# Two graph layers on one core: layer 0's softmax steps for two groups at once, and layer 1's running sums through TensorE and ScalarE

## The reference, cut to what matters

```python
# layer 0, per edge (row, col), 8 heads of 32
scores = sum(Q[row] * K[col], -1) / sqrt(32) * cutoff
attn   = softmax(scores, over the 8 heads)
aggr   = segment_sum(xn[col] * w_phys + gate * attn * V[col], row)      # then @ wo
# layer 1, per edge, 4 heads of 64
e   = leaky_relu(h_l[row] + h_r[col], 0.2)
m   = segment_max(e, row)
ex  = exp(e - m[row])
out = segment_sum(ex * h[col], row) / (segment_sum(ex, row) + 1e-16)
```

## Time and profile before

| | us |
|---|---|
| median of three runs | 2322.39 |
| lowest, highest | 2319.65, 2326.3 |
| the profiled execution, its own time | 2321.69 |
| its span, first to last instruction | 2319.9 |

### The profile page before, as it was taken

One profiled execution on the slowest core, in us unless ns is written; L12 is line 12 of the kernel. 1 busy time (PEld: TensorE's weight loads), 2 busy tenths in 40 slices (PEclk: granted clock), 3 DMA queues, 4 the chain that ended last, 5 costly groups with the idle time before them and its releaser, 6 DMA issues.

```text
span 2319.9 us, 42068 instructions
## 1 busy us (share of the span) xinstructions
PE 1961.0 (85%) x9839; PEld 1426.4 (61%) x9840; DVE 1784.6 (77%) x4372; ACT 1479.1 (64%) x5220; POOL 1409.6 (61%) x1393
## 2 busy tenths in 40 slices
PE   5999999999958899998988889837777877877874
PEld 3777777777747677777777777624444444544542
DVE  5655444444359999998999999667999989999987
ACT  1585555555567777777777777446666666666660
POOL 0377777666776666665666664247666666666660
PEclk9999999999989999999999999977999989998997
DMA  8534444333389888888889882034433333343311
GB/s 279 160 133 144 157 146 146 138 138 131 113 291 301 299 290 292 298 293 280 296 290 308 291 296 76 19 93 113 110 107 107 105 108 100 105 110 104 106 32 56
DMA packets 162185, 403.69 MB, mean 174 GB/s; under 512 B 46887, under 2 KB 59099, under 8 KB 162108
## 3 DMA queue, kind: packets, MB, share of 16 engines
q0 software_dynamic: 79360, 276.09, 36.8%
q1 hardware_dynamic: 82748, 126.67, 17.4%
HBM read 343.89 MB, written 84.72 MB: 185 GB/s over the span
## 4 chain that ended last, share of the span: by engine, by line
PE 39%; DVE 28%; issue 16%; DMA 8%; ACT 4%; DVEq 4%; POOL 2%; SPq 0%; ACTq 0%; POOLq 0%
PE ps L1405 15%; DMA arena<-sorted_edges 6%; DVE gmx L1297 5%; PE ps L1391 4%; PE ps L1518 3%; PE ps L1521 3%; DVE arena L1329 3%; PE ps L1456 3%; PE ps L1533 2%; DVE work L1292 2%; DVE sc L1139 2%; DVE arena L1125 2%; DVEq L350 2%; PE ps L1643 2%; DVE arena L1132 2%
## 5 line engine op out<-in xcount | busy, mean ns | idle before, releaser
L630 POOL DMA_INDIRECT arena<-node_row,idxC x464 | 485.6, 1047 | 233.2 <-issue 136.8
L563 POOL DMA_INDIRECT sorted_edges<-work,pos_i x416 | 405.5, 975 | 236.5 <-issue 118.9
L1405 PE MATMUL ps<-w_sb,arena 128*128 128x256 f32 x1664 | 388.7, 386 | 0.2 <-ACT arena L674 0.2
L1643 PE MATMUL ps<-arena,hq 128*128 128x260 f32 x928 | 279.3, 428 | 96.2 <-DVE work L1292 92.8
L1069 DVE TENSOR_TENSOR work<-ps,b_bc 128x512 f32<-128x512 f32 x208 | 143.6, 691 | 273.6 <-PE ps L1405 273.6
L1405 PEld LDWEIGHTS ps<-w_sb,arena 128*128 128x128 f32 x1664 | 307.5, 190 | 72.2 <-issue 32.5
L585 POOL DMA_INDIRECT work<-node_kvx,idxB x232 | 245.7, 1059 | 154.4 <-DVE arena L1156 54.2
L585 POOL DMA_INDIRECT arena<-node_kvx,idxB x232 | 244.1, 1052 | 144.2 <-issue 51.2
L684 ACT ACTIVATE work<-work 128x256 f32<-128x256 f32 x416 | 187.5, 500 | 209.5 <-DVE work L1069 209.4
L1518 PE MATMUL ps<-arena,work 128*128 128x256 f32 x928 | 256.5, 400 | 59.1 <-issue 52.1
L1297 DVE TENSOR_REDUCE gmx<-ps 128x4 f32<-128x1024 f32 x232 | 282.5, 1218 | 28.4 <-PE ps L1618 28.4
(11 more groups left out here) (216 smaller groups left out, 3786.1 us busy)
## 6 DMA issues: line engine op xcount, KB each, us to landing
arena<-sorted_edges SPq DMA_DIRECT2D x232, 260.0 KB, 4.7
work<-sorted_rows SPq DMA_DIRECT2D x58, 256.0 KB, 3.6
arena<-in_edge_attr SPq DMA_DIRECT2D x25, 512.0 KB
node_kvx<-arena SPq DMA_DIRECT2D x24, 384.0 KB, 2.5
arena<-node_row,idxC POOLq DMA_INDIRECT x464, 3.3
sorted_edges<-work,pos_i POOLq DMA_INDIRECT x416, 2.5
sorted_edges<-arena SPq DMA_DIRECT2D x25, 260.0 KB
sorted_edges<-arena SPq DMA_DIRECT2D x1, 6240.0 KB
```

The costliest lines, as they stand in the source:

```text
L563: pool.indirect_dma_start(rec_dram[:, :], bass.IndirectOffsetOnAxis(ap=pos_i[:, 4 * q + c:4 * q + c + 1], axis=0), recA[:, q % 8, c, :], N ...
L630: pool.indirect_dma_start(row1_g[:, st.slot(16), j, :], None, row1_dram[:, :], bass.IndirectOffsetOnAxis(ap=idxC[:, batch(st).slot(4), st. ...
L1405: ins = pe.matmul(ps[:, 5 + t, half * H:(half + 1) * H], hidT[:, r, m, half, t * P:(t + 1) * P], w2_sb[:, m, :], start=m == 0, stop=m == 1)
L1643: ins = pe.matmul(agg1[r], oneh1[:, r16, j, :], msg1[:, r, j, :], start=j == 0, stop=j == GJ - 1)
```

## The change

Layer 0: `reciprocal`, the attention product and the maximum run once for two groups (an even step takes the maximum of the pair, the odd step after it the other two), the four exponentials of a pair come together on ScalarE in every second step, `msgA` and the final sum come one step later, the rings of the small tiles grow from two to four, and `msgP` gets a ring of four (two slots lie in tiles that are no longer read). The tile numbers are loaded four at a time, twice in a turn, instead of eight at once. Loading a record waits for ScalarE's scaling also.

Layer 1: VectorE no longer adds to `acc1` and no longer scales it. TensorE adds the accumulator itself, as a third matmul with the identity into the same PSUM tile; ScalarE copies the result back, and where the group is the last of a batch it does so in four pieces of 65 columns, each scaled by the next batch's `mscale`. TensorE and ScalarE now load tile numbers for this, VectorE no longer does. VectorE makes the one-hot matrix of a group's second half in one instruction; ScalarE makes the first half alone. `msg1` has a ring of eight. TensorE sums with a lag of 15 (13 before), ScalarE copies with a lag of 17.

```diff
-        def tiles_of(eng, k, lag, count=8):
+        def tiles_of(eng, k, lag, first):
             _, values = nc.values_load_multi_w_load_instructions(
-                gt_i[0:1, bass.ds(k * 8 + (16 - lag), count)], ...
+                gt_i[0:1, bass.ds(k * 8 + (FRONT - lag + first), 4)], ...
 ...
             def load_rec(st):
                 if not st.first(8):
                     sp.wait_ge(s("msgP_ready"), st.n - 7)
+                    sp.wait_ge(s("qk_cut"), st.n - 7)
 ...
             # ScalarE, layer0
-                e = st.back(4)
-                if e.real():
+                if st.u % 2 and st.back(4).real():
+                    e = pair0(st.back(4))
                     act.wait_ge(s("sc_ready"), e.n + 1)
 ...
-                    for j in range(GJ):
-                        ins = act.activation(pe_[:, r, j, :], sc[:, r, j, :], ACT.Exp, ...
+                    for r in (st.back(5).slot(4), st.back(4).slot(4)):
+                        for j in range(GJ):
+                            ins = act.activation(pe_[:, r, j, :], sc[:, r, j, :], ACT.Exp, ...
 ...
             # ScalarE, layer1
+                if st.u % 8 == 0:
+                    act_tiles[17] = tiles16(ACT_ENGINE, st.k, 17, st.u // 8)
+                d = st.back(17)
+                if d.real():
+                    act.wait_ge(s("agg1_ready"), d.n + 1)
+                    to = acc1[:, bass.ds(act_tiles[17][st.u % 8], 1), :].rearrange("p a n -> p (a n)")
+                    if d.u % BG == BG - 1 and not d.end():
+                        k = batch(d).back(-1)
+                        act.wait_ge(s("mscale"), k.n + 1)
+                        for h in range(NH1):
+                            ins = act.activation(to[:, h * HE:(h + 1) * HE], agg1[d.slot(2)][:, h * HE:(h + 1) * HE],
+                                                 ACT.Copy, scale=mscale[:, k.slot(2), h:h + 1])
+                        ins.then_inc(s("acc1_done"), 1)
+                    else:
+                        act.copy(to, agg1[d.slot(2)]).then_inc(s("acc1_done"), 1)
 ...
-                    for j in range(GJ):
-                        act.activation(away[:, st.slot(2), j, :], iota1[:, :], ACT.Abs, ...
+                    act.activation(away[:, h.slot(2), 0, :], iota1[:, :], ACT.Abs, ...
 ...
             # VectorE, layer0: lags a 3, b 4, m 5, c 7 (before: a 3, b 4, c 6)
+                if not both_in and b.real():
+                    e = pair0(b)
+                    re = m.slot(4)
+                    dve.wait_ge(s("exp0"), e.n + 1)
+                    dve.reciprocal(prec[:, :, :], psum_[:, re:re + 2, :]).then_inc(s("prec"), 1)
 ...
+                if both_in and a.real():
+                    r0 = b.slot(4)
                     dve.wait_ge(s("qk_cut"), na + 1)
-                    dve.tensor_reduce(smax[:, ra, :], sc[:, ra, :, :], AX.X, ALU.max, negate=True).then_inc(
-                        s("sc_ready"), 1)
+                    dve.tensor_reduce(smax[:, r0:r0 + 2, :], sc[:, r0:r0 + 2, :, :], AX.X, ALU.max,
+                                      negate=True).then_inc(s("sc_ready"), 1)
 ...
             # VectorE, layer1
-                    tiles[8] = tiles16(DVE, st.k, 11, 0)
 ...
-                    dve.tensor_tensor(acc, acc, agg1[c.slot(2)], ALU.add).then_inc(
-                        s("acc1_done"), 1)
 ...
+                    dve.tensor_scalar(oneh1[:, st.slot(16), 1, :], iota1[:, :], srcC[:, b.slot(4), g, 1:2], None,
+                                      ALU.is_equal)
 ...
             # TensorE, layer1
+                if st.u % 8 == 0:
+                    pe_tiles[15] = tiles16(PE, st.k, 15, st.u // 8)
+                d = st.back(15)
 ...
+                    if not d.first(1):
+                        pe.wait_ge(s("acc1_done"), n)
+                    pe.matmul(agg1[r], ident[:, :],
+                              acc1[:, bass.ds(pe_tiles[15][st.u % 8], 1), :].rearrange("p a n -> p (a n)"),
+                              start=False, stop=True).then_inc(s("agg1_ready"), 1)
```

More of the change, by code:

```diff
@@ L56, in real, with end @@
         return not isinstance(self.k, int) or 0 <= self.n < self.total
+    def end(self):
+        return isinstance(self.k, int) and self.n == self.total - 1
     def first(self, count):
@@ L156, in gnn_kernel @@
         ones = sb("ones", [P, P])
-        w1_sb = sb("w1_sb", [P, H])
+        mlp_only = sb("mlp_only", [P, 4, H])
+        w1_sb, b2_bc, lnw_bc, lnb_bc = (mlp_only[:, i, :] for i in range(4))
         w2_sb = sb("w2_sb", [P, 2, H])
@@ L276, in gnn_kernel @@
                       for v in (NT * (H + HR), NT * (H + HR) + NB * ME))
+        at_same = NT * (H + HR) + 2 * NB * ME
+        same = work[:, at_same:at_same + NB]
         apart = carve(NB * ME * ME).rearrange("p (b e f) -> p b e f", b=NB, e=ME)
@@ L379, in batch, with pair0, msgP_of @@
             return Step(st.k, st.u // BG, 16 // BG, NB)
+        def pair0(st):
+            return Step(st.k, st.u // 2, 4, NG // 2)
+        def msgP_of(st):
+            r = st.slot(4)
+            return msgP[:, r, :, :] if r < 2 else mlp_only[:, 2 * r - 4:2 * r - 2, :]
         def pair(st):
@@ L804, in _ @@
             act.wait_ge(s("hr_parts"), 2)
+            act.wait_ge(s("same"), 1)
             act_tiles = {}
@@ L863, in layer1 @@
                                  own.rearrange("p a q n -> p (a q) n")).then_inc(s("hl_set"), 1)
-                e = b.back(3)
-                if g == 0 and e.real():
+                e = b.back(2)
+                if g == 3 and e.real():
                     r = e.slot(2)
@@ L871, in layer1 @@
                     act.wait_ge(s("mdiff"), e.n + 1)
-                    if not e.first(2):
-                        act.wait_ge(s("acc1_scaled"), e.n - 1)
-                    act.activation(mscale[:, r, :], mdiff[:, r, :], ACT.Exp).then_inc(s("mscale"), 1)
-            run(act, NG, 16, 9, layer1)
+                    act.activation(mscale[:, r, :], mdiff[:, r, :], ACT.Exp,
+                                   scale=same[:, bass.ds(e.n, 1)]).then_inc(s("mscale"), 1)
+            run(act, NG, 16, 17, layer1)
         @block.vector
@@ L1158, in layer0 @@
+                if m.real():
+                    if not both_in:
+                        dve.wait_ge(s("attn"), pair0(m).n + 1)
+                    if not m.first(2):
+                        dve.wait_ge(s("agg0_ready"), m.n - 1)
+                    dve.tensor_tensor(heads(msgA[:, m.slot(2), :, :]), heads(kvx_g(m)[:, :, H:2 * H]),
+                                      attn[:, m.slot(2), :, :].unsqueeze(3).to_broadcast([P, GJ, NH0, HD0]),
                                       ALU.mult).then_inc(s("msgA_ready"), 1)
-                if a.real():
+                if both_in and a.real():
+                    r0 = b.slot(4)
@@ L1326, in layer1 @@
                         dve.wait_ge(s("exp1"), batch(m).n + 1)
-                    if not m.first(2):
-                        dve.wait_ge(s("agg1_ready"), m.n - 1)
-                    dve.tensor_tensor(msg1[:, m.slot(2), :, :].rearrange("p c (h d) -> p c h d", d=HE),
+                    if not m.first(8):
+                        dve.wait_ge(s("msg1_used"), m.n - 7)
+                    dve.tensor_tensor(msg1(m).rearrange("p c (h d) -> p c h d", d=HE),
                                       row1_g[:, m.slot(16), :, 0:HR].rearrange("p c (h d) -> p c h d", d=HE),
```

155 lines of the change are left out of this document (71 added, 84 removed).

## The result

The changed kernel takes 2434.41 us (median of four runs, 2432.01 to 2440.77), the kernel before 2322.38 us (four runs beside it): ratio 1.0485, 95% interval 1.0469 to 1.0501. It is slower by 112 us; forecast were 2231 us.

The account below looks back on a forecast made before the run. VectorE was taken to lead both layers, with TensorE close to the bound in layer 0. From 2321.7 us, 56 saved in layer 0 and 39 in layer 1, with 4 lost at the end, gave 2231 us; range 2165 to 2290.

Parts of the forecast that it names:

- The signs that the prediction had set for being wrong in layer 1: Layer 1: VectorE's maximum waiting for TensorE, TensorE for ScalarE's copies, and a clock lower than 0.92.
- The new wait in SyncE's record load: Layer 0: SyncE's record load also waits for ScalarE's scaling, which VectorE's maximum has long waited for; priced at nothing.
- as long as ScalarE comes to them in time: Layer 0: condition under which VectorE's 1.79 us of products and head sum cover the reciprocal's wait for four exponentials.
- the forecast 3.18: Layer 0: predicted period in us a group, from 3.42; 56 us saved, bounds 3.06 and 3.36.
- TensorE's 3.06: Layer 0: TensorE's us a group from a turn of 24.5 us, loads of four included, half-speed passes mostly gone.
- Two loads then cost VectorE between nothing and 0.1 us each: nothing taken: Layer 0: a load of four, 0.9 us shorter, hides beside VectorE's products, where 0.84 us stuck out before.
- the half-speed stretch: Layer 0: TensorE's passes behind a load of eight run at the lower clock; 1.04 us a turn, taken as mostly gone.
- two engines are close to the bound: Layer 0 before the change: TensorE's turn of eight groups, 25.5 us, is as long as VectorE's 25.0 + 0.84.
- Nothing, if it hides behind other work: Layer 1: three cases for the TensorE-ScalarE hand-over: nothing, 0.2 us, or more in a rival; 2.92 us a group taken, 39 saved.
- The round in layer 1 is the new bound: Layer 1 rival: uncovered ScalarE masks, load and copy add 0.85 us a group, giving 3.55 and 2377 us; chance 0.09.
- bounds of 2.72 to 3.10: Layer 1: range in us a group around the forecast 2.92, from 86 us saved to 2 lost.
- The end: Last groups pass through TensorE and ScalarE in turn, with lags of 15 and 17: 4 us lost, bounds 0 and 10.

Follow-up runs that it names:

- e4: Changed kernel with AHEAD = 1 for 2: in layer 0 ScalarE copies a record's indices one step later; 2381.34 us, ratio 1.0246.
- e2: Changed kernel with ScalarE's copy of layer 1's batch indices in the batch's third step, not its first; 2302.98 us, ratio 0.9909.
- e5: Changed kernel with both the later index copy of e2 and the AHEAD = 1 of e4; 2251.97 us, ratio 0.9687.
- e15: e9 with AHEAD = 2 as before; 2299.74 us, ratio 0.9891.
- e8: Kernel before with AHEAD = 1 alone; 2320.29 us, ratio 0.9977.
- e9: Kernel before with AHEAD = 1 and layer 0's tile numbers loaded four at a time, nothing paired; 2263.45 us, ratio 0.9739.
- e13: e7 without TensorE's lookups of Q in layer 0 (scores of wrong rows); 2169.89 us, ratio 0.9340.
- e14: e9 without TensorE's lookups of Q in layer 0; 2262.12 us, ratio 0.9732.
- e12: e7 without layer 1's lookups of the accumulator tile, always using the first tile; 2202.67 us, ratio 0.9473.
- e6: e5 with ScalarE's second mask line of a layer 1 batch moved to the end of the batch's second step; 2219.91 us, ratio 0.9539.
- e7: e6 with layer 1's register loads on ScalarE and TensorE four values at a time instead of eight; 2214.45 us, ratio 0.9514.
- e11: e7 with both halves of layer 1's one-hots on ScalarE, none on VectorE; 2248.22 us, ratio 0.9677.
- e10: e7 with the indices one step later than in the changed kernel instead of two; 2215.46 us, ratio 0.9524.
- e16: e7 with layer 0's tile numbers loaded two at a time on VectorE and TensorE; 2190.43 us, ratio 0.9415.

## Why the prediction was wrong

Of the 203 us between the forecast and the measurement e4 gives back 53, in layer 0, and e2 131, in layer 1; both together (e5) 182. Of the 21 that are left 14 are layer 1's 2.98 us for 2.92. The signs that the prediction had set for being wrong in layer 1 were seen: VectorE's maximum waits for TensorE (189.1 us), TensorE for ScalarE's copies (146.5), and the clock fell to 0.88.

**Layer 0, the new wait on SyncE.** "The new wait in SyncE's record load is for a scaling that VectorE's maximum has long waited for: nothing". That wait itself did end ahead of the old one in the trace, by 1.7 us. The step that failed is beside it: the sum had a turn for each engine and the transfers, but not the ring of buffers through the records. The condition that it set itself, "as long as ScalarE comes to them in time", was not followed up. A slot is free at `msgP` of group n - 8; the record lands and is copied some 5 us later; the exponentials stand behind that copy in ScalarE's queue, VectorE's reciprocal behind the exponentials, and the next `msgP` behind that. With AHEAD = 2 this spans three steps: it holds the period at 3.32 us unpaired (e15) and 3.43 paired. In e15's trace, where ScalarE waits for a record, the copy starts 5.5 us after the `msgP` that freed the slot, and the `msgP` of three groups on ends 4.2 us after that (medians): 9.7 us, 3.24 a step. Since the kernel before ran at 3.42 anyway, the ring cost next to nothing there (e8), and its row of waits, 76.7 us on ScalarE, looked like idle time of an engine that does not bind. With the ring out of the way the forecast 3.18 came out to the digit (e4). That digit is luck: the 0.1 that was put on TensorE's 3.06 was half of today's 0.2, an allowance and no sum of prices, and gives 3.16, not 3.18.

**Layer 0, what gained.** With the ring open the sum there is right as a whole and wrong in its parts. "Two loads then cost VectorE between nothing and 0.1 us each: nothing taken" and "What may go is the half-speed stretch ... taken as mostly gone" both hold then: VectorE does not wait behind its load in e4, a load takes TensorE 1.002 us, the clock is 0.99 to 1.00. But the pairing stood first, as 0.18 us a group saved on VectorE, and the comparison was never drawn that the prediction's own numbers allow: without the pairing VectorE stands at 3.13 and TensorE, with loads of four, at 3.06 either way, so that the pairing could be worth 0.07 at most. It was worth nothing here: the loads of four alone give 3.16 (e9), and the pairing then only exchanges VectorE for TensorE and its stalls as the bound (e13, e14). The two-engine tie was read correctly ("two engines are close to the bound"); relieving one of two is worth little until the other is relieved, and e13 against e14 shows VectorE's saving, 0.17 us, once it is. One reading of it is too large: of VectorE's 2.3 us a turn the prediction gave 0.84 to its own load and "the rest", 1.5, to a late TensorE, for which the kernel before waits 19.3 us in 27 turns (line L1125, 660 to 1440 us), 0.7 a turn.

On the loads the prediction set 0.99 us by the row of SyncE against 1.3 us by the page "Runtime: NRT & Kernel Launch" of the Trainium skill, section "The ~15µs preamble/postamble breakdown". That section speaks of the register loads from HBM that the runtime puts ahead of a kernel, not of a kernel's loads out of SBUF. The trace has 1.002: the price by the value held.

**Layer 1, the round.** "Nothing, if it hides behind other work; the same 0.2 us as in layer 0 ... I take 2.92 us" failed; of its three cases the third came true, the rival "The round in layer 1 is the new bound", at 3.53 us a group where it had 3.55. The nearness of the two numbers is luck: the rival had ScalarE's masks and load ahead of the copy and not the largest part, and its time, 2377 us, is 57 short because layer 0's 56 did not come. Of the 0.74 us between the changed kernel and e12, 0.56 went with the index copy's wait for VectorE's maximum (e2), and in it what the lower clock cost; the second mask has 0.13 (e6), the load of eight at most 0.02 (e7, not shown), the rest of the added lookups 0.04 (e12). These shares hold for this order of repairs: no run takes the masks out and leaves the wait. The wait that decided is a line of the change that stands in no step of the prediction, and what is queued behind it was not asked. Queued behind it were the masks and the scaled copies for which TensorE was already standing. Without that wait the period is 2.97, inside the bounds of 2.72 to 3.10 and 0.05 from the forecast.

**The price of the parts.** VectorE's one-hot took 0.28 us in length, as its row had said, and e11 shows the exchange worth 0.15 us a group. The end cost 4.2 us, forecast 4, within bounds of 0 and 10 that were a guess. So the operations were priced well; what was missed were two rounds of waits, one in each layer. With both opened (e5) the kernel takes 2252 us, 21 from the forecast.

**The page on ScalarE.** The rule of the Trainium skill's page "ScalarE: Activation LUTs", section "Rules for kernel authors", that additions and products belong on VectorE spoke for the rival, and the change as it stands is slower. In price the trace agrees: the four scaled pieces take ScalarE 0.91 us, the same scaling took VectorE 0.42. But layer 1 with the sums on TensorE and ScalarE, and half of the one-hots on VectorE, is faster than before once the index copy is moved: 2.97 us a group in e2, 3.09 before. The loss came from the order in the queue, not from the engine.

## What to carry to other kernels

When a change moves work into an in-order queue, list each wait that the diff adds, and for each what stands behind it in that queue and who waits for that; a wait "for the ring" of a small tile is a wait like any other, and moving a 0.2 us copy two steps later was worth 131 us here (e2); one step did as well (e10). Before you shorten a step, walk every ring of buffers through all its engines and divide by the steps it spans: a ring that shows as harmless waiting today can be the floor of the shorter step. Where two engines tie, relieve one alone only to measure; and split a stall that drains TensorE until it fits into the work queued ahead of it.

## What the runs showed of the hardware

A register load's time goes by the values: on TensorE 0.546 us for two, 1.002 for four and 1.937 for eight, some 0.23 a value and 0.08 beside; VectorE and ScalarE are a little quicker (0.968 for four, 1.756 for eight). Halving the size of a load is therefore nearly free in sum. Whether it cuts TensorE's idle time depends on the work around it: without the pairing it was 50.4 us in layer 0 behind loads of eight and 28.1 behind loads of four (e9), with the pairing 49.4 behind loads of four (e4) and 23.8 behind loads of two (e16).

TensorE's granted clock in layer 1 was 0.92 before, 0.88 in the changed kernel and 0.98 in e2, which has the changed kernel's instructions in another order; TensorE's longest waits there were 2.7, 3.6 and 2.0 us. Two passes behind an idle stretch of 3.54 us ran at the lower of the two levels, 1.23 us for 0.60: that wait cost 0.63 us more than its length.
